# Forty-two products of the identity with zeros per turn, put into TensorE's order in a four-layer transformer kernel

## The chip, the cores and the metric

The kernel runs on one core of one Trainium2 chip. The metric is the device time of one execution in microseconds (us), so less is better. Before the change it is 3342.41 us, the median of three executions (3336.08 to 3346.99). TensorE is called PE here, VectorE DVE and ScalarE ACT. SyncE (SP) issues the DMAs, and GpSimd (POOL) only clears a few tiles at the start.

## The reference, cut to what matters

The input is 16 sequences of 256 tokens with 128 features. Eight stages follow each other, each one a layer norm, the stage and a residual:

```python
x = x + _L0_attn_ref(_layernorm(x, axis=-1), ...)   # causal attention, 16 heads of 8
x = x + _L0_ffn_ref(_layernorm(x, axis=-1), ...)    # 8 experts, top 2, with a capacity
x = x + _L1_attn_ref(_layernorm(x, axis=-1), ...)   # causal attention
x = x + _L1_ffn_ref(_layernorm(x, axis=-1), ...)    # 4-head attention with shared keys, then 8 experts
x = x + _L2_attn_ref(_layernorm(x, axis=-1), ...)   # linear attention
x = x + _L2_ffn_ref(_layernorm(x, axis=-1), ...)    # causal attention, then a gated MLP
x = x + _L3_attn_ref(_layernorm(x, axis=-1), ...)   # attention whose weights come from arccos
x = x + _L3_ffn_ref(_layernorm(x, axis=-1), ...)    # three blocks of quantised linears with low-rank terms
```

## The kernel before, in words

Work is cut into eight passes of two sequences (512 tokens), with the features on the 128 partitions. A pass has a front half (first two layers: `causal0`, `moe0`, `causal1`, `mqa`, `moe1`) and a back half (`linear`, `causal2`, `mlp`, `arccos`, `qlora` and three blocks). There are two regions, `one` and `two`. Each has its own SBUF and four PSUM banks of its own (`one_ps`, `two_ps`). The program has three parts. "fronts" runs the front halves of the first two passes, one in each region. "both" is a loop of six turns; a turn runs the front half of one pass in region `one` beside the back half of an earlier pass in region `two`. "backs" runs the last two back halves.

Every engine's order is written out. Each stage is a generator per engine (`headed_pe`, `mqa_act`, ...) that yields between steps, and `weave` takes steps from the two halves in turn by the numbers of `PE_RUNS`, `ACT_RUNS` and `DVE_RUNS`:

```python
    for i, steps in enumerate(runs):
        for _ in range(steps):
            next(halves[i % 2], None)
```

An engine therefore waits at the head of its own list, and what stands behind the waiting instruction waits too. A step begins with its semaphore waits. All hand-overs between engines go through semaphores that count up.

The places that the change and the prediction touch, by line of the kernel before: L557 and L564 are the two matmuls of a layer norm. L658, L659 and L649 are the projections. L766 and L772 are scores for a softmax's maximum, and DVE's L797 takes the maximum. L837, L843 and L848 are the scores, with ACT's L933 as their exponential, and L862 and L865 multiply by the values. L883 and L910 are linear attention. L1001 and L1008 end an attention stage. L1124, L1132, L1148, L1150 and L1164 are the 4-head attention `mqa`, and L1095 and L1099 are its end. L1257 and L1275 are the arccos attention, whose ACT passes are L1320 and L1322 and whose sums are DVE's L1330. L1595 to L1646 are the experts of `moe0`. L1437 and L1448 spread the routing weights of `moe1`, and L1710, L1717 and L1723 are its experts. L1821 and L1826 are the linears of the blocks. Most of these matmuls take fp32 operands, and each of those stands as two records in the trace: four matmuls of 128 columns are "x8".

`clear_ps` (L894) is a product of the bf16 identity with zeros. It is used four times at the program's start, ahead of everything.

Of the kernel before, what the change touches and what calls it, by code (L numbers as in the profile page):

```python
# [33 lines left out]
P = 128  # L34
# [78 lines left out]
class Signal:  # L113
# [12 lines left out]
    def before(self, turn):  # L126
# [53 lines left out]
    ),  # L180
    "both": (
# [5 lines left out]
    ),  # L187
    "backs": (
# [50 lines left out]
        ("block", "block0"), ("block", "block1"), ("block", "block2")]  # L239

# [239 lines left out]
def build(nc, x_dram, w_dram, qw_dram, out_dram):  # L480
    cols, width = columns()
    with ExitStack() as ctx:
        def sb(name, shape, dt=F32):
            return ctx.enter_context(nc.sbuf_tensor(name, shape, dt))
# [15 lines left out]
        zero_bf, spare = sb("zero_bf", [P, 1], BF16), sb("spare", [P, 1])  # L500
        max_rows = sb("max_rows", [P, GROUPS], F32R)
# [16 lines left out]
        def C(name):  # L518
            return W("const", name)
# [1345 lines left out]
        def run(eng, runs, stage_of, before_back=None):  # L1865


            def half(h, parts, turn):
                return in_turn(parts, turn, {kind: lambda t, s, f=f: f(eng, h, t, s) for kind, f in stage_of.items()})
# [52 lines left out]
        @block.gpsimd  # L1922
        def _(pool):

            for h in (one_front, two_front):
                nc.gpsimd.memset(h.v18[:], 1.0).then_inc(consts_ready, 1)
                nc.gpsimd.memset(h.negm[:], 0.0).then_inc(consts_ready, 1)
                nc.gpsimd.memset(h.v33[:], 1.0).then_inc(consts_ready, 1)
            nc.gpsimd.memset(zero_bf[:], 0.0).then_inc(consts_ready, 1)
            nc.gpsimd.memset(spare[:], 0.0).then_inc(out_stored, 16)  # L1930

        CONSTS = 19
# [11 lines left out]
        def _(pe):  # L1944
            pe.wait_ge(loaded["const"], 16)
            pe.wait_ge(consts_ready, CONSTS)
            for region in (one, two):
                for bank in (2, 3):
# [3 lines left out]
                     "moe1": moe1_pe, "mlp": mlp_pe, "arccos": arccos_pe, "block": block_pe}, lora_pe)  # L1952
# [147 lines left out]
```

## Time and profile before

| | |
|---|---|
| median of three executions | 3342.41 us |
| lowest and highest | 3336.08 and 3346.99 us |
| the profiled execution, span from first to last instruction | 3337.4 us |
| PE busy | 2641.8 us, 79% |
| ACT busy | 1912.7 us, 57% |
| DVE busy | 1763.9 us, 53% |
| mean granted clock of PE | 0.795 of full speed |
| chain that ended last | PE 54%, ACT 19%, DVE 15%, issue 12% |

The profiled execution's own time is its span, 3337.4 us, which is 5.0 us under the median. The row PEclk of the page shows the clock that was granted to PE in each fortieth of the span. It is 1.0 for 2.4 GHz and 0.5 for 1.2 GHz, and figures between are means over both. The chain of work that ended last goes back from the last instruction to what released it, step by step. Busy shares are means over stages with different limits, so a stretch is read by its own row.

### The profile page before, as it was taken

What the parts mean: (1) busy time and instruction counts of PE and PEld (TensorE: products, weight loads), DVE (VectorE), ACT (ScalarE), POOL (GpSimd) and SP (SyncE); (2) the same over time, 40 slices, a digit from 0 to 9 for tenths busy, and PEclk for the clock granted to TensorE, in tenths of its full rate; (3) what the DMA queues carried; (4) which work ended last, traced back from release to release, by engine and by line L of the source; (5) the groups of instructions that cost most, each with busy time, mean ns of one, the idle gap of its engine ahead of it and who ended that gap; (6) DMA issues with size and microseconds to landing.
All of it is one profiled execution on the core that took longest, in us unless ns stands there. A gap on an engine that the chain in (4) does not pass through costs nothing.

```text
span 3337.4 us, 46425 instructions
## 1 busy us (share of the span) xinstructions
PE 2641.8 (79%) x18736; PEld 1529.0 (46%) x18736; DVE 1763.9 (53%) x2698; ACT 1912.7 (57%) x1960; POOL 3.6 (0%) x12
## 2 busy tenths in 40 slices
PE   8999999777997789877898688986889868897215
PEld 4666456343563435534355344553445534453102
DVE  5463574545656355553555545654455544563524
ACT  2433435875358753586445864468534685447994
POOL 0000000000000000000000000000000000000000
PEclk7997989659896588966899668986779867987557
DMA  3000000000000000000000000000000000000000
GB/s 128 2 1 1 20 1 1 1 1 8 1 1 1 1 8 1 1 1 0 8 1 1 1 0 8 2 1 1 0 5 2 1 1 0 4 1 1 0 0 6
DMA packets 4561, 18.68 MB, mean 6 GB/s; under 512 B 608, under 2 KB 864, under 8 KB 3808
## 3 DMA queue, kind: packets, MB, share of 16 engines
q1 hardware_dynamic: 4320, 15.38, 1.2%
q8 instruction: 162, 2.65, 0.3%
q14 instruction: 79, 0.65, 0.1%
HBM read 13.28 MB, written 2.10 MB: 5 GB/s over the span
## 4 chain that ended last, share of the span: by engine, by line
PE 54%; ACT 19%; DVE 15%; issue 12%; DVEq 0%; DMA 0%; ACTq 0%; SPq 0%
ACT back_cosines L1320 6%; PE one_ps L1164 2%; PE two_ps L1275 2%; PE one_ps L862 2%; PE two_ps L910 2%; ACT back_cosines L1322 2%; PE one_ps L1710 2%; DVE back_nsum L1330 2%; PE one_ps L1717 2%; ACT L1320 2%; PE one_ps L766 1%; PE one_ps L1723 1%; DVE back_cosines L1393 1%; ACT L1862 1%; PE two_ps L862 1%
## 5 line engine op out<-in xcount | busy, mean ns | idle before, releaser
L1320 ACT ACTIVATE back_cosines<-back_cosines 128x2048 f32<-128x2048 f32 x256 | 472.2, 1899 | 0.5
L933 ACT ACTIVATE front_scratch<-one_ps 128x1152 f32<-128x1152 f32 x168 | 171.5, 1021 | 225.0 <-PE one_ps L848 224.8
L1322 ACT ACTIVATE back_cosines<-back_cosines,wts 128x2048 f32<-128x2048 f32 x128 | 252.4, 1994 | 41.1 <-DVE back_cosines L1393 40.9
L1330 DVE TENSOR_REDUCE back_nsum<-back_cosines 128x8 f32<-128x2048 f32 x64 | 144.4, 2281 | 234.0 <-ACT back_cosines L1320 234.0
L797 DVE TENSOR_REDUCE front_negm<-one_ps 128x8 f32<-128x1024 f32 (+1 forms) x168 | 204.4, 1220 | 56.6 <-PE one_ps L772 55.5
L837 PE MATMUL one_ps<-ident_bf,mask_q 128*128 128x256 bf16 x480 | 93.3, 302 | 80.5 <-ACT front_scratch L933 69.3
L696 ACT ACTIVATE back_cosines<-two_ps,wts 128x512 fp32r<-128x512 f32 x28 | 19.3, 688 | 224.1 <-PE two_ps L910 224.1
L766 PE MATMUL one_ps<-front_qkr 32*128 32x128 f32 (+1 forms) x896 | 136.5, 414 | 14.1 <-issue 8.9
L1393 DVE TENSOR_SCALAR back_cosines<-two_ps 128x2048 f32<-128x2048 f32 x56 | 128.2, 2290 | 28.5 <-PE two_ps L1257 28.3
L933 ACT ACTIVATE back_cosines<-two_ps 128x1152 f32<-128x1152 f32 (+1 forms) x84 | 86.0, 1024 | 92.0 <-PE two_ps L848 92.0
L766 PEld LDWEIGHTS one_ps<-front_qkr 32*128 32x128 f32 x896 | 96.6, 274 | 88.5 <-DVE front_negm L797 46.3
L1275 PE MATMUL two_ps<-back_cosines,back_vs 128*18 128x256 f32 x896 | 79.5, 505 | 69.0 <-DVE back_vs L1342 69.0
L862 PE MATMUL one_ps<-front_scratch,one_v 128*18 128x256 f32 x896 | 116.7, 424 | 6.1 <-DVE front_split_parts L704 5.7
L772 PE MATMUL one_ps<-mask_q,ident_bf 128*128 128x512 bf16 (+1 forms) x360 | 119.4, 428 | 0.0
L843 PE MATMUL one_ps<-front_qkr 32*128 32x256 f32 (+1 forms) x896 | 105.8, 328 | 0.0
L797 DVE TENSOR_REDUCE back_cosines<-two_ps 128x4 f32<-128x1024 f32 (+1 forms) x84 | 97.9, 1216 | 8.8 <-PE two_ps L772 8.6
L837 PEld LDWEIGHTS one_ps<-ident_bf,mask_q 128*128 128x128 bf16 x480 | 39.2, 103 | 132.7 <-ACT front_scratch L933 92.1
L700 DVE TENSOR_SCALAR front_scratch<-one_ps,wts 128x512 fp32r<-128x512 f32 x77 | 57.4, 746 | 71.6 <-PE one_ps L865 56.0
L910 PE MATMUL two_ps<-back_cosines,two_v 128*18 128x128 f32 x896 | 77.8, 376 | 20.9 <-DVE back_split_parts L704 20.6
L1164 PEld LDWEIGHTS one_ps<-front_v,front_scratch 128*128 128x128 f32 x448 | 85.0, 291 | 13.0 <-issue 13.0
L953 DVE TENSOR_TENSOR back_cosines<-two_ps,wts 128x768 f32<-128x768 f32 (+1 forms) x84 | 72.6, 864 | 34.8 <-PE two_ps L883 34.8
L843 PEld LDWEIGHTS one_ps<-front_qkr 32*128 32x128 f32 x896 | 71.3, 208 | 42.1 <-issue 42.1
(630 smaller groups left out, 5795.1 us busy)
## 6 DMA issues: line engine op xcount, KB each, us to landing
wts<-w_dram SPq DMA_DIRECT2D x1, 4184.0 KB, 15.3
front_xin<-x_dram SPq DMA_DIRECT2D x8, 256.0 KB, 4.2
out_dram<-back_z SPq DMA_DIRECT2D x8, 256.0 KB, 2.1
wts<-w_dram SPq DMA_DIRECT2D x1, 1736.5 KB, 19.1
wts<-w_dram SPq DMA_DIRECT2D x1, 1199.0 KB, 5.3
wts<-w_dram SPq DMA_DIRECT2D x1, 1152.0 KB, 16.5
wts<-w_dram SPq DMA_DIRECT2D x3, 256.0 KB, 5.8
wts<-w_dram SPq DMA_DIRECT2D x1, 516.5 KB, 4.8
```

The costliest lines, as they stand in the source:

```text
L766: nc.tensor.matmul(h.ps[:, j, gi * keys:(gi + 1) * keys], h.q4r[rows(j, QUAD), g0 + gi, b * SEQ + qt * P:b * SEQ + (qt + 1) * P], h.k4r[ro ...
L797: nc.vector.tensor_reduce(into, h.ps[:, js, :].rearrange("p j (g k) -> p j g k", k=keys), AX.X, ALU.max, negate=True).then_inc(h.max_done. ...
L843: nc.tensor.matmul(h.ps[:, k, into], h.k4r[rows(j, QUAD), g, keys], h.q4r[rows(j, QUAD), g, queries], start=False, stop=False, skip_group_ ...
L862: nc.tensor.matmul(h.ps[rows(j, V2), 3, b * SEQ:(b + 1) * SEQ], h.v18[:, 2 * b, GROUPS * j + g, :], h.probs[:, e % 2, k * HEADW:k * HEADW ...
L910: last = nc.tensor.matmul(h.ps[rows(j, V2), 3, b * SEQ + t * P:b * SEQ + (t + 1) * P], h.v18[:, 2 * b + t, GROUPS * j + g, :], h.probs[:, ...
L933: nc.scalar.activation(h.probs[:, e % 2, 0:n * HEADW].rearrange("p (k c) -> p k c", c=HEADW), h.ps[:, 0:n, 0:HEADW], ACT.Exp, scale=float( ...
L1164: last = nc.tensor.matmul(h.ps[:, 3, c:c + MV1], h.probs[:, (e - 1) % 2, w:w + P], h.v33[:, 2 * b + kt, :], start=(kt == 0), stop=(kt == 1 ...
L1275: last = nc.tensor.matmul(h.ps[rows(j, V2), 2 + g2, 0:SEQ], h.vs[:, kt, HPG * g2 + j, :], h.cosines[:, u % 2, w:w + SEQ], start=(kt == 0), ...
L1320: nc.scalar.activation(cosines, cosines, func, scale=scale).then_inc(h.arc_pass.sem, 1)
L1322: nc.scalar.activation(cosines, cosines, func, scale=scale, bias=C(bias)).then_inc(h.arc_pass.sem, 1)
L1330: nc.vector.tensor_reduce(h.nsum[:, kt, :].rearrange("p (g2 j) -> p j g2", g2=2), h.cosines[:, u % 2, kt * 4 * TOK:(kt + 1) * 4 * TOK].rea ...
L1393: nc.vector.tensor_scalar(h.cosines[:, u % 2, kt * 4 * TOK:(kt + 1) * 4 * TOK].rearrange("p (j t) -> p j t", j=HPG), h.ps[:], CLIP, CLIP_L ...
```

## The change

A tile of zeros `zero_f` (fp32) is added, and a table `IDLE_WORK` that says for a step of a half how many products of the fp32 identity with zeros PE issues ahead of it, into which bank and which quarter of it. They always go to bank 3, mostly its last quarter. An entry has two counts: the first are issued before the other half gets its turn, the second after it. Entries of (0, 0) issue nothing and only add a yield. 22 counts are above zero, and they sum to 42 for a front and a back half together: 18 in the front half, 24 in the back half. The numbers of `PE_RUNS` are written anew so that the added yields move nothing. A product has no wait and raises no semaphore.

```diff
 PE_RUNS = {
     "fronts": (
-        1, 1, 1, 1, 1, 1, 1, 1, 1, 1, 2, 2, 2, 1, 2, 2, 5, 1, 5, 2, 1, 1, 2, 1, 2, 1, 2, 1, 2, 1, 2, 1, 2, 2, 2,
+        2, 2, 2, 2, 2, 2, 2, 2, 2, 2, 2, 2, 3, 1, 2, 3, 5, 1, 6, 2, 2, 1, 4, 1, 4, 1, 3, 1, 2, 1, 4, 1, 3, 3, 2,
...
+IDLE_WORK = {
+    "front": {
+        1: (2, 3, (0, 0)), 2: (3, 3, (0, 0)), 3: (3, 3, (0, 0)), 4: (3, 3, (0, 0)), 5: (3, 3, (0, 0)), 9: (3, 3,
+        (0, 0)), 21: (3, 3, (0, 0)), 22: (3, 3, (0, 0)), 23: (3, 3, (0, 4)), 24: (3, 3, (0, 0)), 25: (3, 3, (0,
...
+        3, (0, 0)), 126: (2, 3, (0, 0)), 133: (3, 3, (2, 2)), 134: (3,
+        3, (0, 4)), 135: (3, 3, (0, 0)), 136: (3, 3, (0, 0)), 137: (3, 3, (0, 0)), 138: (3, 3, (0, 0)), 139: (2,
...
+        zero_f = sb("zero_f", [P, 1])
...
+        def with_idle_work(h, steps, work):
+
+            step = 0
+            while True:
+                if step in work:
+                    bank, quarter, times = work[step]
+                    for part, n in enumerate(times):
+                        if part:
+                            yield
+                        for _ in range(n):
+                            nc.tensor.matmul(h.ps[:, bank, quarter * P:(quarter + 1) * P], C("ident"),
+                                             zero_f[:].broadcast_to([P, P]), start=True, stop=True, skip_group_check=True)
+                try:
+                    next(steps)
+                except StopIteration:
+                    return
+                step += 1
+                yield
...
             def half(h, parts, turn):
-                return in_turn(parts, turn, {kind: lambda t, s, f=f: f(eng, h, t, s) for kind, f in stage_of.items()})
+                steps = in_turn(parts, turn, {kind: lambda t, s, f=f: f(eng, h, t, s) for kind, f in stage_of.items()})
+                if idle_work:
+                    return with_idle_work(h, steps, idle_work["front" if parts is FRONT else "back"])
+                return steps
...
+            nc.gpsimd.memset(zero_f[:], 0.0).then_inc(consts_ready, 1)
...
-        CONSTS = 19
+        CONSTS = 20
```

Lines of the kernel from L237 on stand 48 or 49 lines further down in the changed kernel, and from the new helper on 71 or 72 lines further down. The product itself is L1924 there. Three places in PE's order follow. The first is in the loop, early in a turn: `one` takes the maxima of `causal0` while `two` is in its linear attention. PE's order before:

```order
L910 MATMUL two_ps<-back_cosines,two_v 18x128 x6
L876 REGISTER_ALU
L883 MATMUL two_ps<-back_qkr 128x128 x4
L910 MATMUL two_ps<-back_cosines,two_v 18x128 x6
L763 REGISTER_ALU
L766 MATMUL one_ps<-front_qkr 128x128 x8
```

The same place in the changed kernel:

```order
L959 MATMUL two_ps<-back_cosines,two_v 18x128 x6
L1924 MATMUL two_ps<-zero_f,wts 128x128 x2
L925 REGISTER_ALU
L932 MATMUL two_ps<-back_qkr 128x128 x4
L959 MATMUL two_ps<-back_cosines,two_v 18x128 x6
L812 REGISTER_ALU
```

Two products stand between the two linear-attention steps, and all else keeps its place. The second place is in the loop too, a little later, where `two` leaves linear attention (`two_ps` with L1008) and `one` is in its `causal0` scores. PE's order before:

```order
L843 MATMUL one_ps<-front_qkr 128x128 x3
L848 MATMUL one_ps<-front_maxTr,max_rows 128x128 x3
L1008 MATMUL two_ps<-back_xn,wts 128x512
L834 ISA
L837 MATMUL one_ps<-ident_bf,mask_q 128x2x128 x3
```

And in the changed kernel:

```order
L892 MATMUL one_ps<-front_qkr 128x128 x3
L897 MATMUL one_ps<-front_maxTr,max_rows 128x128 x3
L1057 MATMUL two_ps<-back_xn,wts 128x512
L1924 MATMUL one_ps<-zero_f,wts 128x128 x4
L883 ISA
L886 MATMUL one_ps<-ident_bf,mask_q 128x2x128 x3
```

Four products stand ahead of the next score set. The third place is late in a turn, where `one` ends `mqa` (L1164, L1095, L1099) and `two` is in the last value products of arccos (L1275). PE's order before:

```order
L1164 MATMUL one_ps<-front_v_64,front_scratch 128x33 x8
L1275 MATMUL two_ps<-back_cosines,back_vs 18x256 x16
L1156 REGISTER_ALU
L1164 MATMUL one_ps<-front_v_64,front_scratch 128x33 x8
L1095 MATMUL one_ps<-wts,front_scratch 128x128 x4
L1099 MATMUL one_ps<-front_xn,wts 128x512
L1275 MATMUL two_ps<-back_cosines,back_vs 18x256 x16
L564 MATMUL one_ps<-front_sq,wts 128x512
```

And in the changed kernel:

```order
L1213 MATMUL one_ps<-front_v_64,front_scratch 128x33 x8
L1324 MATMUL two_ps<-back_cosines,back_vs 18x256 x16
L1924 MATMUL two_ps<-zero_f,wts 128x128 x4
L1205 REGISTER_ALU
L1213 MATMUL one_ps<-front_v_64,front_scratch 128x33 x8
L1144 MATMUL one_ps<-wts,front_scratch 128x128 x4
L1148 MATMUL one_ps<-front_xn,wts 128x512
L1924 MATMUL one_ps<-zero_f,wts 128x128 x2
L1324 MATMUL two_ps<-back_cosines,back_vs 18x256 x16
L1924 MATMUL one_ps<-zero_f,wts 128x128
L613 MATMUL one_ps<-front_sq,wts 128x512
```

Four, two and one products come in at three points. On ACT, DVE and SP every row stands where it stood, and POOL has one more memset at the start.

## Rows read from the trace of the kernel before

**Rows 1.** The page: its span, PE's clock in forty slices, the chain by engine.
```profile
span 3337.4 us, 46425 instructions
...
PEclk7997989659896588966899668986779867987557
...
PE 54%; ACT 19%; DVE 15%; issue 12%; DVEq 0%; DMA 0%; ACTq 0%; SPq 0%
```

**Rows 2.** Stretches: length; busy PE, PEld, DVE, ACT, POOL; clock; DMA share, GB/s.
```profile
1248.00:1278.70 30.70, 26.98 (x192) 16.02 (x191) 19.71 (x26) 2.47 (x4) 0.00 (x0) 0.50 0.00 1
1278.70:1405.00 126.30, 118.01 (x1085) 76.27 (x1084) 68.59 (x129) 63.73 (x93) 0.00 (x0) 1.00 0.00 1
1405.00:1411.80 6.80, 5.75 (x19) 3.46 (x20) 4.58 (x4) 4.91 (x4) 0.00 (x0) 0.50 0.00 0
1415.20:1469.80 54.60, 38.15 (x243) 19.65 (x243) 28.20 (x29) 52.57 (x33) 0.00 (x0) 0.50 0.00 1
...
1558.60:1565.40 6.80, 4.41 (x22) 1.75 (x26) 5.24 (x9) 1.06 (x2) 0.00 (x0) 0.50 0.00 0
...
1585.90:1592.70 6.80, 5.48 (x8) 2.19 (x8) 4.42 (x6) 5.29 (x6) 0.00 (x0) 0.50 0.00 0
...
309.30:346.80 37.50, 36.48 (x130) 25.96 (x130) 11.56 (x42) 10.60 (x14) 0.00 (x0) 0.50 0.00 0
...
1534.70:1551.80 17.10, 17.10 (x82) 14.87 (x82) 5.86 (x8) 15.31 (x10) 0.00 (x0) 0.50 0.00 1
...
1496.00:1550.00 54.00, 37.54 (x144) 24.21 (x143) 16.35 (x27) 53.55 (x39) 0.00 (x0) 0.53 0.00 0
```

**Rows 3.** Timeline of PE, start and length in us: fp32 matmuls of 128 columns.
```profile
330.85 1.89 PE L1437 MATMUL one_ps<-wts,front_wtok 128*16 128x128 f32 x8
...
1364.96 1.05 PE L1638 MATMUL one_ps<-wts,front_parts 128*128 128x128 f32 x8
1365.85 1.06 PE L1623 MATMUL one_ps<-front_scratch,wts 128*128 128x128 f32 x8
...
1578.04 1.05 PE L1437 MATMUL one_ps<-wts,front_wtok 128*16 128x128 f32 x8 [1.54 <-DVE front_wtok L1570]
```

**Rows 4.** The chain in 1248 to 1279: shares by line, then start, length, what.
```profile
by line: PE two_ps L910 29.1%; PE one_ps L766 14.4%; PE two_ps L883 13.5%; PE one_ps L772 11.4%; PE two_ps L1001 9.7%; DVE back_split_parts L704 9.5%; issue 6.2%; DVE back_cosines L953 3.6%; PE two_ps L920 2.8%; ACT back_cosines L696 2.3%; 
...
1248.93 1.05 PE two_ps L910 x12
1249.98 0.62 PE two_ps L883 x4
```

**Rows 5.** Timeline of PE at full clock; idle before in brackets.
```profile
1282.05 0.50 PE L837 MATMUL one_ps<-ident_bf,mask_q 128*128 128x256 bf16 x3 [0.18 <-ACT front_scratch L933]
...
1361.03 1.05 PE L1623 MATMUL one_ps<-front_scratch,wts 128*128 128x128 f32 x8
...
1367.35 1.06 PE L1406 MATMUL two_ps<-wts,back_xn 128*128 128x8 f32 x8 [0.45 <-DVE back_xn L622]
```

**Rows 6.** Timelines of PE and of ACT at the start of the `mqa` probabilities.
```profile
1529.87 1.23 PE L1148 MATMUL one_ps<-front_qk 32*128 32x256 f32 x4 [1.63 <-DVE front_maxTr L704]
...
1533.40 1.00 ACT L1186 ACTIVATE front_scratch<-one_ps 128x1024 f32<-128x1024 f32 x1
```

**Rows 7.** The chain from 1557 to 1592: start, length, what.
```profile
1557.20 2.28 DVE back_nsum L1330
...
1560.30 1.13 PE one_ps L1095 x4
...
1562.10 2.08 PE one_ps L1099 x2
1564.18 2.52 PE two_ps L1275 x32
...
1587.35 2.07 PE one_ps L1710 x2
```

**Rows 8.** Timeline of PE where five products come in ahead of L557.
```profile
1583.78 1.20 PE L1448 MATMUL one_ps<-front_maxTr,expert_rows 16*128 16x512 f32 x4 [0.91 <-ACT front_qk L1481]
```

More of the change, by code:

```diff
@@ L239 @@
         ("block", "block0"), ("block", "block1"), ("block", "block2")]
+IDLE_WORK = {
+    "front": {
[22 rows of a table added]
+    },
+    "back": {
[18 rows of a table added]
+    },
+}
 def weave(runs, halves):
@@ L1863, in table, with run @@
             in_table[0] = name
-        def run(eng, runs, stage_of, before_back=None):
+        def with_idle_work(h, steps, work):
[15 more added lines that the diff above has]
+                yield
+        def run(eng, runs, stage_of, before_back=None, idle_work=None):
             def half(h, parts, turn):
-                return in_turn(parts, turn, {kind: lambda t, s, f=f: f(eng, h, t, s) for kind, f in stage_of.items()})
+                steps = in_turn(parts, turn, {kind: lambda t, s, f=f: f(eng, h, t, s) for kind, f in stage_of.items()})
+                if idle_work:
+                    return with_idle_work(h, steps, idle_work["front" if parts is FRONT else "back"])
+                return steps
             table(None)
@@ L1951, in _ @@
             run(pe, PE_RUNS, {"norm": norm_pe, "causal": headed_pe, "linear": headed_pe, "mqa": mqa_pe, "moe0": moe0_pe,
-                     "moe1": moe1_pe, "mlp": mlp_pe, "arccos": arccos_pe, "block": block_pe}, lora_pe)
+                     "moe1": moe1_pe, "mlp": mlp_pe, "arccos": arccos_pe, "block": block_pe}, lora_pe, IDLE_WORK)
         @block.scalar
```

67 rows, old and new, of tables (IDLE_WORK, PE_RUNS) are left out of this document.

## The prediction

> **What bounds the kernel now.** I read the page first, its row of PE's clock and its chain [rows 1]. PE is 54% of the chain over a span of 3337.4 us, and the clock wanders between 5 and 9 tenths with the same pattern in every turn of the loop. So the question is where PE is both on the chain and at the low level. I took the turn from 1213.8 to 1623.4 as the sample, cut it where the granted clock changes, and asked for busy times by stretch [rows 2]. The reader is to see three kinds. From 1278.7 to 1405.0 the clock is 1.00 (2.4 GHz) and PE is busy 118.01 of 126.30 us: nothing can be won there, and PE is the bound. In 1415.2 to 1469.8 and in 1496.0 to 1550.0 the clock is at or near 0.50 (1.2 GHz), but ACT is busy 52.57 of 54.60 and 53.55 of 54.00: a faster PE would wait for ACT. Only the third kind pays: 1248.0 to 1278.7, 1405.0 to 1411.8, 1558.6 to 1565.4 and 1585.9 to 1592.7 all have 0.50, PE busy four fifths of the time or little less, and ACT and DVE with room. Then I looked up each insertion in the changed order, found the instructions around it in the trace, and read the idle time in front of the one behind it.
>
> **What a product costs.** The trace has no fp32 product of 128x128 with 128 columns of zeros, but real ones of that shape. Four of them are "x8". L1638 starts at 1364.96 and L1623 behind it at 1365.85: 0.89 us for four, 0.22 us each at 2.4 GHz [rows 3]. L1437, of the same columns, takes 1.89 us at 0.50 and 1.05 at 1.00 for four, 0.84 us more, so 0.43 us each at 1.2 GHz. A product behind which PE waits anyway costs nothing; behind which it doesn't, its full price. It has no wait and signals nobody, so nothing else queues. 42 per turn are 9.2 us at full clock and 18.1 us at the low level. Zero operands could only make this cheaper in power, not in time: I use the price of the real ones.
>
> **Part by part, one turn.** What comes back is half of PE's time in a stretch that turns from 1.2 to 2.4 GHz, as far as PE is on the chain. Which stretches turn can't be read from the trace of before; I bound each.
>
> A, 1248.0 to 1278.7: two products behind L910 with nothing idle there, since L883 starts at 1249.98 where L910 ends [rows 4]. They cost 2 x 0.43 = 0.86 us for certain. PE's lines make 81% of the chain (29.1, 14.4, 13.5, 11.4, 9.7 and 2.8%), 24.8 of 30.7 us. At full clock throughout that would be 12.4 less, but DVE has 19.71 us of work, so at most 11.0 come back. At the low end nothing does. Work of the same kind let the clock fall at 1248.0, so I expect a short lift: a fifth of the 11.0, 2.2, less 0.86, and I take +1.5. This is the least sure term, from -0.9 to +10.1.
>
> B, 1405.0 to 1411.8: one product shortly before (0.22). PE is busy 5.75 us there; full clock returns at most 2.9. I take +0.8.
>
> C, the single product at 1461 (low, 0.43): ACT hides its cost and most of its gain. +0.5, from 0 to 2.
>
> D, eight products ahead of L1148 at 1529.87, where PE is idle 1.63 us for DVE [rows 6]. At 1.2 GHz they take 3.4 us, so L1148 starts 1.8 us later. ACT's exponential behind it starts at 1533.40, with ACT full before it; the score set is two groups of some 1.2 us, so it ends near 1532.3 before and near 1534.1 after; 0.7 us would show if the clock stays low, and none if it rises. The gain is bounded by ACT, which stays full until 1550.0 [rows 2]. I take 0, from -0.7 to +3 (only if PE were still fast for the last L1164 and L1275 behind ACT's end).
>
> E, 1558.6 to 1565.4: four products at 1555.7, in front of L1164, whose result DVE wants only after its 2.28 us sum (L1330) [rows 7], so their 0.88 us are hidden. If they hold the clock up, L1095 (1.13), L1099 (2.08) and the first half of L1275 run at full clock: 4.4 us busy become 2.2. Two more products ahead of L1275 cost 0.44. +1.6, from -1.1 to +1.8.
>
> F, 1585.9 to 1592.7: L1710, L1717 and L1710 of `moe1` stand on the chain at 1.2 GHz, the first with 2.07 us [rows 7]; PE is busy 5.48 us [rows 2], and at full clock half of it, 2.7, comes back. The five products at 1581.8 fill 1.1 us against 0.91 us idle [rows 8]: 0.2 lost. +2.2 before that, from -0.2 to +2.7 with it.
>
> G, the products in the long stretch at full clock: four with 0.18 us idle to fill, 0.88 - 0.18 = 0.70; two ahead of L837 in the `causal2` scores and two ahead of L1623 with none idle, 0.44 each; single ones ahead of L1406, where 0.45 us are idle [rows 5], and ahead of L1222, alike, hidden. PE is the bound there: -1.6, almost certain.
>
> The rest of the turn's products (1566 to 1578) stand where PE is idle longer than they take, as the 1.54 us ahead of L1437 [rows 3]: 0. What is late next where a low stretch goes is DVE in A, and nothing new in E and F, whose chain is PE, ACT and DVE by turns.
>
> Sum of a turn: 1.5 + 0.8 + 0.5 + 0 + 1.6 + 2.2 - 0.2 - 1.6 = 4.8 us. Six turns: 29 us. In "fronts", eight products stand ahead of the `mqa` of `two`, whose low stretch 309.3 to 346.8 is PE alone (36.48 of 37.50 us) with no ACT to wait for [rows 2]; at most 18 us come back there, and the other products cost some 3. I take +5 net. In "backs" most of the low time is ACT's, so 0. In all 34 us: 3337.4 - 34 = 3303.4 for the profiled execution, and since the median of before stands 5.0 us above it, 3308 us.
>
> **Two rules of the Trainium skill.** From 1534.7 to 1551.8 PE is busy 17.10 of 17.10 us, and the clock is 0.50 all the while [rows 2]. The Trainium skill, page "TensorE: Matmul & The Clock Gate", section "Why this matters for your kernels", says that PE kept busy continuously gets to full clock. The trace differs: by that rule this stretch would have been fast already; by the row a PE that never idles can stay at the low level, so filling idle time is no promise of a faster clock. The same page, section "PE-mode transpose", says that transposes, products with an identity, don't count as busy for the clock in the same way. No run shows whether a plain matmul on the identity falls under it; by that rule the case of the slower rival below would hold.
>
> **The rivals.**
> Slower: the products don't raise the clock, or raise it where ACT holds the chain. Then only prices are left. Per turn: A 0.86, B 0.22, E 0.44 and one more of 0.22, F 0.2, G 1.6, a last 0.4 for C and D, together 4.0 us, six turns 24 us; "fronts" and "backs" have 84 products, at the same 0.095 us a product 8 us. 3342.4 + 32 = 3374 us. It decides as soon as a turn gets back less than 4.0 us from the clock. For it: in 1534.7 to 1551.8 a full PE is not enough, and A starts with a sure loss. Against it: E and F lie right behind a stretch at 1.00 and need it held only a little longer.
> Much faster: A stays at 2.4 GHz to its end and so does the `mqa` in "fronts". That is 8.6 us more a turn, 52 us, and up to 13 more in "fronts": 3308 - 65 = 3243 us. For it: PE is 81% of the chain there. Against it: the same work let the clock fall.
> No change: E and F give 3.8 us a turn, A and G take 2.5 of it back, the rest moves into waits: 1.3 x 6 = 8 us, 3334 us. The edit does move PE's order as it says, so that it does nothing is no case of its own.
>
> **How the numbers follow.** A measurement of this kernel tells a change from none beyond about 0.3%, that is outside 3332 to 3352 us. I give the forecast 0.53, the much faster case 0.14, no change 0.14, slower 0.19. Faster is 0.53 + 0.14 = 0.67. The forecast's own range is 3285 to 3330 us: A alone moves a turn by -2.4 to +8.6, the others by about 2 either way, and they don't all fall out alike in six turns. The range for 8 in 10 goes on to 3262 below, half way into the much faster case, and to 3360 above, half way into the slower one.
>
> **What the profile after would show.** The products, L1924, with 672 records in all, mean spacing 0.11 us a record at full clock. If I am right: in a turn the granted clock is 1.00 where F stands (the first L1710 takes about 1.1 us, not 2.07), and where E stands (L1099 about 1.1 us). The stretch of A is shorter by 1 to 4 us, with DVE waited for more often. ACT's full stretches are as long as before, whatever the clock does in them. The long full-clock stretch is longer by 1 to 2 us. The mean granted clock is above 0.82. I am wrong to the slow side if the clock is low in E and F as before, and to the fast side if A is at 1.00 throughout.

## The result, and the profile after

The changed kernel takes 3356.78 us, the median of seven executions (3353.01 to 3364.34), against 3342.41 us of before on the same chip (seven, 3334.25 to 3347.15). The ratio is 1.0041 with a 95% interval from 1.0026 to 1.0056. It is slower by 14 us, and the forecast was 3308.

The page of the changed kernel answers to [rows 1]: its span, PE's busy time, the clock in forty slices, and the chain by engine.

```profile
span 3358.6 us, 47776 instructions
...
PE 2709.0 (81%) x19408; PEld 1621.0 (48%) x19408; DVE 1765.0 (53%) x2698; ACT 1913.1 (57%) x1960; POOL 3.6 (0%) x13
...
PEclk7998879769896688966889668996789867988558
...
PE 57%; ACT 18%; DVE 14%; issue 11%; DVEq 0%; DMA 0%; ACTq 0%; SPq 0%
```

PE is busy 67 us longer, and its share of the chain went up from 54% to 57%. The mean granted clock is 0.810 against 0.795 (the forecast asked for more than 0.82), so the products did raise the clock, and the kernel is slower all the same. The question is therefore where the clock rose and where it fell.

I cut the changed kernel where its clock changes, as in [rows 2] (columns: stretch, length, busy PE, PEld, DVE, ACT and POOL, granted clock, DMA share, GB/s). The copy of `handed` into `back_x` (L638 before, L687 now) is a good mark for the start of a turn. Two turns start at 816.8 and 1225.3.

```profile
816.80:845.30 28.50, 23.66 (x174) 13.11 (x174) 19.12 (x25) 14.19 (x19) 0.00 (x0) 0.92 0.03 10
845.30:872.60 27.30, 24.31 (x187) 13.70 (x185) 17.85 (x23) 1.41 (x3) 0.00 (x0) 0.50 0.00 1
1225.30:1244.70 19.40, 15.81 (x76) 8.00 (x77) 10.06 (x14) 13.50 (x18) 0.00 (x0) 0.85 0.05 15
1244.70:1292.50 47.80, 43.91 (x299) 26.14 (x298) 29.49 (x37) 4.07 (x6) 0.00 (x0) 0.50 0.00 1
1292.50:1422.20 129.70, 121.01 (x1115) 79.27 (x1114) 71.08 (x131) 64.28 (x92) 0.00 (x0) 1.00 0.01 1
...
1548.50:1569.00 20.50, 20.50 (x115) 16.05 (x111) 5.87 (x8) 14.97 (x10) 0.00 (x0) 0.50 0.00 1
1569.00:1575.80 6.80, 4.29 (x30) 3.59 (x31) 6.60 (x8) 0.60 (x1) 0.00 (x0) 1.00 0.00 0
1592.90:1606.60 13.70, 11.58 (x36) 5.22 (x35) 7.11 (x9) 8.52 (x10) 0.00 (x0) 1.00 0.00 0
```

The last row is F (the letters A to G are the stretches of the forecast), and the one ahead of it is the first half of E. F is at 1.00 now, as the forecast wanted. In E the low stretch has moved and is not gone. Here it is just behind the row, and L1148 (L1099 of [rows 7], 2.07 us there) takes 1.30 us in this turn and 1.97 in the second one (a stretch, then PE's timeline):

```profile
1575.80:1579.20 3.40, 3.40 (x29) 1.67 (x31) 1.37 (x4) 0.63 (x1) 0.00 (x0) 0.50 0.00 0
...
1159.21 1.97 PE L1148 MATMUL one_ps<-front_xn,wts 128*128 128x512 f32 x2 [0.69 <-ACT front_xn L1153]
...
1574.96 1.30 PE L1148 MATMUL one_ps<-front_xn,wts 128*128 128x512 f32 x2 [0.69 <-ACT front_xn L1153]
```

Over the six turns L1148 takes 1.30 to 2.07 us, where the forecast wanted 1.1. F's first product takes 1.12 or 1.13 us in all six, but in two of them the clock falls again for 3.4 us soon behind it.

The first four rows above are A in two turns. In the first of them PE's clock holds for 28.5 us and A's low stretch is 27.3 us. In the second it falls after 19.4 us, and the low stretch is 47.8 us. The trace of before has the same two patterns, the long one in its last turn only (2445.6):

```profile
1219.20:1248.00 28.80, 24.07 (x176) 13.18 (x176) 19.43 (x25) 14.20 (x19) 0.00 (x0) 0.91 0.03 11
...
2445.60:2466.50 20.90, 17.39 (x86) 8.64 (x86) 10.85 (x15) 13.52 (x18) 0.00 (x0) 0.83 0.01 2
2466.50:2510.90 44.40, 40.50 (x287) 23.44 (x285) 28.68 (x36) 3.44 (x5) 0.00 (x0) 0.50 0.00 1
```

I call this an early fall. From the mark to A's first L1001 (L1050 now), the six turns take, in us:

| | turn 1 | 2 | 3 | 4 | 5 | 6 |
|---|---|---|---|---|---|---|
| before | 55.9 | 56.1 | 56.1 | 56.1 | 56.1 | **61.6** |
| changed kernel | **64.3** | 57.3 | **62.7** | **62.2** | **62.1** | 57.3 |

Bold turns fell early. So A costs 1.2 us in an undisturbed turn, and an early fall 5 us more. The changed kernel has four of them in its profile where before has one.

The account of the two profiled executions, taken between the same DVE instructions, closes: A has +23.9 us over the six turns (7 of price, about 17 of early falls by the table), G has +8.0 (1.7 in an undisturbed turn), all the rest of the loop has -18.1, fronts +1.9, backs +5.5. The sum is +21.2 us, the difference of the spans.

Two products in A and what follows them (columns: start, length, engine, line, operation, tiles, idle time before):

```profile
1260.47 1.05 PE L959 MATMUL two_ps<-back_cosines,two_v 128*18 128x128 f32 x12 [0.74 <-DVE back_split_parts L753]
1261.45 1.22 PE L1924 MATMUL two_ps<-zero_f,wts 128*128 128x128 f32 x4
1262.61 0.69 PE L932 MATMUL two_ps<-back_qkr 32*128 32x128 f32 x4
```

From the first product to L932 (L883 of [rows 4]) it is 1.16 us, so 0.58 us each at 1.2 GHz, not the 0.43 taken from [rows 3]. The chain through E and F has them too (start, length, what):

```profile
1574.96 1.30 PE one_ps L1148 x2
1576.26 0.85 PE one_ps L1924 x4
...
1595.17 1.31 PE two_ps L1924 x10
...
1603.41 0.86 PE one_ps L1759 x2
```

The first L1759 (L1710 of [rows 7], 2.07 us there) takes 0.86 us, so F did get its clock. But about 3.3 us of products (10.2% of the chain from 1575 to 1608) stand on the path in this stretch, where the forecast put 0.6. Standing on the path is not the same as costing time, though: from the start of L613 (L564 before) at 1580.4 to that of the first L1759 it is 20.6 us in all six turns, against 20.8 in four turns of before and 21.7 in the other two.

### The profile page after: what moved, and what is told of

Same layout as the page of the kernel before. It is cut to its first block, busy times and chain, and to the rows that moved or that the text cites. A ratio compares the mean times of both kernels' runs of the same rounds, so it can differ in the third digit from the quotient of the medians.

```text
span 3358.6 us, 47776 instructions
## 1 busy us (share of the span) xinstructions
PE 2709.0 (81%) x19408; PEld 1621.0 (48%) x19408; DVE 1765.0 (53%) x2698; ACT 1913.1 (57%) x1960; POOL 3.6 (0%) x13
## 4 chain that ended last, share of the span: by engine, by line
PE 57%; ACT 18%; DVE 14%; issue 11%; DVEq 0%; DMA 0%; ACTq 0%; SPq 0%
ACT back_cosines L1369 6%; ACT back_cosines L1371 2%; PE one_ps L1213 2%; PE two_ps L959 2%; PE one_ps L911 2%; PE two_ps L1324 2%; PE one_ps L815 2%; DVE back_nsum L1379 2%; PE one_ps L1766 2%; ACT L1369 2%; PE one_ps L821 2%; PE one_ps L1759 2%; PE one_ps L1772 2%; PE two_ps L606 1%; ACT L1911 1%
## 5 line engine op out<-in xcount | busy, mean ns | idle before, releaser
L745 ACT ACTIVATE back_cosines<-two_ps,wts 128x512 fp32r<-128x512 f32 x28 | 19.3, 688 | 245.0 <-PE two_ps L959 245.0
L815 PE MATMUL one_ps<-front_qkr 32*128 32x128 f32 (+1 forms) x896 | 144.1, 432 | 11.6 <-issue 8.9
L749 DVE TENSOR_SCALAR front_scratch<-one_ps,wts 128x512 fp32r<-128x512 f32 x77 | 57.5, 747 | 75.8 <-PE one_ps L914 60.3
L621 ACT ACTIVATE back_sq<-two_ps 128x512 f32<-128x512 f32 x49 | 29.3, 597 | 103.6 <-PE two_ps L606 102.8
```

The lines of the kernel that those rows point to most:

```text
L815: nc.tensor.matmul(h.ps[:, j, gi * keys:(gi + 1) * keys], h.q4r[rows(j, QUAD), g0 + gi, b * SEQ + qt * P:b * SEQ + (qt + 1) * P], h.k4r[ro ...
```

## The experiments

Each kernel was timed in five rounds beside the kernel before on the same chip. The ratio is to that. "Count" means the entries of `IDLE_WORK`. The order of all other instructions is that of the changed kernel, except where a diff adds some. Line numbers of these kernels lie one to nine above those of the changed kernel. Two theories are weighed. By the price theory a product costs its time or wins clock where it stands, and nothing else moves. By the timing theory how long A stays fast also depends on when a turn arrives, so what is won or lost anywhere moves the early falls.

### One group of products at a time

`only_g`, `only_ef`, `ef_loop`, `bcd_loop`, `a_only`, `behind_l910` and `turn_start` keep one group and set the other counts to zero; `a_filled` has thirty products of its own in A and ahead of it. All but `only_g` and `only_ef` also keep fronts and backs free of products (cut to what matters):

```diff
-                        for _ in range(n):
+                        for _ in range(n if on else 0):
...
-                    return with_idle_work(h, steps, idle_work["front" if parts is FRONT else "back"])
+                    return with_idle_work(h, steps, idle_work["front" if parts is FRONT else "back"], turn.register is not None)
```

**G alone.** 

> Of the products only the ten of a turn in the long stretch at full clock (G). They can bring nothing where they stand. Price theory: plus 1.7 us a turn and 3 us outside the loop, 3342 + 13 = 3355 us, with A as before. Timing theory: 3355 us plus about 6 us for each turn in which A's clock falls early, up to 3391 us.

Measured: 3340.29 us, ratio 1.0003 (0.9987 to 1.0018). Its rows of the long stretch at full clock and of a whole turn:

```profile
1278.70:1408.50 129.80, 120.90 (x1112) 78.92 (x1111) 71.48 (x131) 64.93 (x93) 0.00 (x0) 1.00 0.01 1
...
1219.80:1629.20 409.40, 332.85 (x2360) 193.67 (x2360) 219.44 (x336) 240.14 (x246) 0.00 (x0) 0.80 0.01 2
```

PE is the bound there as in [rows 2], and between the same DVE instructions G takes 1.7 us longer, as forecast. Yet its first five turns take 409.0 to 410.1 us against 409.2 in the usual turn of before (the last turn of each kernel is some 2.6 us shorter behind F). The 1.7 us are given back behind G in most turns: from 196 to 251 us behind the mark it takes 53.5 us in four of the six, where before takes 55.0 to 56.6. Both theories fail here. The price is real and the kernel doesn't pay it.

**B, C and D alone.** 

> Only the ten products of B, C and D, in the loop; eight of them stand ahead of L1148 (D). The prediction gave B +0.8, C +0.5, D 0: 8 us less, ratio 0.998. If ACT holds that part of the turn whatever PE's clock is: 1.000.

Measured: 3332.41 us, ratio 0.9977 (0.9957 to 0.9996). This is the size of the forecast's B, C and D, and the lowest ratio of all that ran. Its turns don't bear out the terms, though. Two take 406.6 us, but `start_and_fronts` (below), whose loop has none of these ten products, has a turn of 406.5 us too, and the fifth turn of before takes 407.1:

```profile
1224.40:1630.90 406.50, 330.32 (x2344) 191.35 (x2344) 219.51 (x335) 240.33 (x246) 0.00 (x0) 0.81 0.01 2
```

Three more turns take 409.1 to 409.6 us, as the usual turn of before. What its profile has less than that of before lies mostly in the last turn, which doesn't fall early (406.8 against 413.4 us).

**E and F alone, with fronts and backs, and in the loop only.** 

> Of the products only those of E and F and the few between them (1555 to 1582 in a turn of the kernel before). Price theory: E and F give 2.0 to 2.5 us a turn and nothing else moves, 3342 - 14 = 3328 us. Timing theory: the same gain of about 14 us, plus about 6 us for every turn in which A's clock falls early; with none 3328, with all six 3364 us. If E and F give nothing by themselves: 3342 us.

> The products of E and F and between them, in the loop only. Where they also stood in fronts and backs, a turn took 406.5 us against 409.2 in the usual turn of before, yet backs took 491 us against 478. If the products in backs are the cost: 6 x 2.7 = 16 us less than before, ratio 0.995, less 5 us of that for each turn whose A falls early beyond the one of before. If backs is longer for another reason: ratio about 1.001, as with the products everywhere.

Measured: 3342.04 us, ratio 1.0025 (1.001 to 1.004), and 3345.67 us, ratio 1.0009 (0.9987 to 1.0031). Here are three turns of the second in a row, and below them the two parts of A in the second and the third turn:

```profile
403.50:810.50 407.00, 334.10 (x2376) 195.14 (x2376) 219.18 (x336) 240.38 (x246) 0.00 (x0) 0.81 0.02 6
810.50:1225.60 415.10, 343.70 (x2376) 201.33 (x2376) 219.91 (x336) 240.47 (x246) 0.00 (x0) 0.78 0.01 2
1225.60:1632.10 406.50, 332.03 (x2376) 195.00 (x2376) 219.49 (x336) 240.35 (x246) 0.00 (x0) 0.81 0.01 2
...
810.50:830.80 20.30, 17.15 (x86) 8.81 (x86) 10.92 (x15) 13.51 (x18) 0.00 (x0) 0.83 0.04 14
830.80:875.20 44.40, 40.51 (x285) 23.54 (x284) 28.64 (x36) 3.57 (x6) 0.00 (x0) 0.50 0.00 1
1225.60:1254.10 28.50, 23.72 (x174) 13.10 (x174) 19.16 (x25) 14.19 (x19) 0.00 (x0) 0.92 0.03 11
1254.10:1281.50 27.40, 23.96 (x186) 13.27 (x182) 18.43 (x24) 2.06 (x3) 0.00 (x0) 0.50 0.00 1
```

This is the clearest picture of the case. The turns take 407.0, 415.1 and 406.5 us, though they have the same instructions; the second falls early. In the profile this repeats every three turns, and the mean over the six is 409.1 us, against 409.7 in before: the gain is nearly gone. What differs at the start of the early turn is when the clock rose: 6.7 us behind the mark at 810.5, 4.6 us behind the one at 1225.6. Where the clock changes doesn't move along with the turn, so a turn that arrives earlier has its high time at other instructions.

How much of a short turn is E and F is read between the same DVE instructions. E's stretch (336 to 346 us behind the mark) takes 9.6 us in all six turns, and 9.4 to 10.3 in before: no gain that can be told from its spread. F's (360 to 381 us) takes 19.3 us in two turns and 20.8 in four, and 21.0 to 21.2 in before. So F gives 1.8 us where the clock stays up for all of it, and 0.2 elsewhere. The turn of 406.5 us is one of the four. Of its 2.7 us under the usual 409.2, 1.5 lie from 193 to 336 us, ahead of the first product of E, and `start_and_fronts` reaches 406.5 with no product of E and F in its loop.

**The two pairs of A.** 

> Only the two products at a turn's start and the two in A behind L910, in the loop. The prediction took A for +1.5 us a turn (a gain). By the profiles so far A is 1.2 us longer with them at either clock: 3342 + 7 = 3349 us, ratio 1.002, and no lift of the clock in A's low stretch. If they do lift it: ratio 0.997 or less. If they also make A fall early: 1.005 and more.

> Only the two products in A behind L910, in the loop. If this pair is the cause: about 20 us slower than before, ratio 1.006, with A 58 us or more from the turn's marker (the copy of handed to back_x) to the first L1001 in most turns, against 56.1. If the other pair is: price alone, 6 x 1.2 = 7 us, ratio 1.002.

> Only the two products at a turn's start, in the loop, ahead of the first L557, where PE is idle 4.55 us. Their price is hidden: if nothing else follows, ratio 1.000. If they are the cause of the 0.76%, because the clock then rises later behind them: ratio 1.004 to 1.006, and the clock at 1.00 from 7 to 8 us behind the marker on, against 4.1 to 4.8 in the usual turn of before.

Measured: both pairs 3363.41 us, ratio 1.0076 (1.005 to 1.0102). Behind L910 alone 3336.32 us, ratio 0.9994 (0.9973 to 1.0015), with A at 57.1 to 57.5 us in every turn: the price of 1.2 us and no lift. At the turn's start alone 3355.31 us, ratio 1.0058 (1.0033 to 1.0083). I had not expected two products in 4.55 us of idle time to cost this. PE's timeline at the seam, of before and of `turn_start`:

```profile
1213.44 1.72 PE L1826 MATMUL two_ps<-back_sq,weff 128*128 128x512 f32 x2
...
1219.71 2.07 PE L557 MATMUL two_ps<-back_x,wts 128*128 128x512 f32 x2 [4.55 <-DVE back_x L638]
```

```profile
1217.75 1.12 PE L1876 MATMUL two_ps<-back_sq,weff 128*128 128x512 f32 x2
1223.61 0.76 PE L1925 MATMUL two_ps<-zero_f,wts 128*128 128x128 f32 x2 [4.73 <-issue]
1226.69 0.80 PE L1925 MATMUL two_ps<-zero_f,wts 128*128 128x128 f32 x2 [2.32 <-issue]
1227.27 1.91 PE L607 MATMUL two_ps<-back_x,wts 128*128 128x512 f32 x2
```

Between the two products PE waits 2.32 us for nothing that the profile shows ("issue"). From the end of the last L1876 to the first L607 it is 6.6 us or more (8.4 here) in all five seams of `turn_start`, and 4.5 to 5.1 us in before. The clock comes up later with it, 7.1 to 7.7 us behind the mark in the five turns that follow, against 4.1 to 4.8 in the first five of before. But the changed kernel has both pairs and no such stall: its seams are 4.6 to 4.8 us. So I ran the pair again behind fronts with their 36 products.

> The two products at a turn's start in the loop, and the 36 products of fronts ahead of it, which only lie before the loop in time and in the code. If the stall between the two products hangs on where the loop's code lies: it is gone, the first L607 starts 4.7 us behind the turn's last L1876 product as in the changed kernel, and the time is 1.000 to 1.002 of before. If it comes of the products themselves: 6.6 us as in turn_start, and 1.006 again.

Measured: 3344.28 us, ratio 1.0012 (0.9997 to 1.0027). Its seam:

```profile
1218.51 1.73 PE L1876 MATMUL two_ps<-back_sq,weff 128*128 128x512 f32 x2
1222.62 1.20 PE L1925 MATMUL two_ps<-zero_f,wts 128*128 128x128 f32 x4 [2.37 <-issue]
1224.93 2.08 PE L607 MATMUL two_ps<-back_x,wts 128*128 128x512 f32 x2 [1.12 <-DVE back_x L688]
```

The stall is gone in all five seams (4.6 to 4.9 us), though the loop's instructions are the same. What changed is only what stands before the loop. The three kernels with this pair and no product in fronts (`turn_start`, `a_only` and `after_loop`, the last two at 6.5 to 6.8 us) stall in every seam, and the four with both (the changed kernel, `no_g`, `after_hold` and this one) in none. That speaks for where the loop's first instructions lie, though no run changed that alone, and why the issue stops is not shown. The difference of 0.46% between the two kernels, whose intervals don't overlap, goes with the stall, and a part of the loss of `a_only` and `after_loop` can be that.

**A filled.** 

> Products only in A and ahead of it, thirty per turn of the loop: 4 ahead of L658 of linear, 2 ahead of the front's q, 1 and 1 after, then 2 at each of eleven places between the groups of L883 and L910. Much-faster rival of the prediction: A stays at 2.4 GHz, up to 11 us a turn back, less some 5 us of price: a turn 6 us shorter, 3342 - 36 = 3306 us. If they can't hold the clock: 22 x 0.43 = 9.5 us a turn of price less the idle time they fill (about 3 us in A): 3342 + 40 = 3382 us, with A's low stretch 27 us or more in every turn.

Measured: 3403.48 us, ratio 1.0178 (1.0164 to 1.0192). A stretch of A, and two places in it:

```profile
1275.70:1305.20 29.50, 26.95 (x178) 17.64 (x172) 15.20 (x16) 1.38 (x2) 0.00 (x0) 0.50 0.00 1
```

```profile
1277.79 1.22 PE L1925 MATMUL two_ps<-zero_f,wts 128*128 128x128 f32 x4
1278.94 1.05 PE L960 MATMUL two_ps<-back_cosines,two_v 128*18 128x128 f32 x12
...
1281.79 1.06 PE L1925 MATMUL two_ps<-zero_f,wts 128*128 128x128 f32 x4
1282.78 0.69 PE L933 MATMUL two_ps<-back_qkr 32*128 32x128 f32 x6
```

PE is busy 26.95 of 29.50 us with products among the work, and the clock is 0.50. So the much faster rival fails even with A filled: A is 11 us longer a turn. The loss is above my 40 us because a product costs 0.50 to 0.58 us at this level, not 0.43.

### The changed kernel with a group taken out

**Without G.** 

> The changed kernel without the ten products of a turn that stand in the long stretch at full clock (the term G). Price theory (only prices and clock gains, each where its products stand): minus 1.7 us a turn and some 3 us outside the loop, 3357 - 13 = 3344 us, and the low stretch inside A stays 41.0 us or more in four of six turns. Timing theory (how long A stays fast depends on when a turn arrives, and G's 1.7 us help to decide that): the low stretch in A is back at 27.3 to 30.7 us in most turns, 3357 - 13 - 24 = 3320 us.

Measured: 3346.18 us, ratio 1.0027 (1.0007 to 1.0048), from 3332.91 to 3370.01. Without G the ratio is 0.14% lower than with it, where the price theory asked for 0.4% and the timing theory for 1.1%, and the intervals overlap. In its profile one turn of six falls early, but twelve executions spread over 37 us, and all of its interval is above 1. So G alone is not what makes the changed kernel slower, and this run shows no more.

**Without both pairs of A.** 

> The changed kernel without the two products in A behind L910 and without the two at a turn's start. Theory that these products themselves make the clock of A fall early: the low stretch in A is 27.3 to 30.7 us in all turns, 3357 - 6 (their price) - 24 = 3327 us. Price theory: 3357 - 6 = 3351 us with four long stretches. Timing theory: between the two; the long stretches come in other turns than in the changed kernel, not in none.

**Without the pair at the start.** 

> The changed kernel without the two products at a turn's start, the pair behind L910 kept. Without both pairs the ratio was 0.9999, with both 1.0041. If the pair behind L910 makes that difference (1.2 us a turn of price and the early falls): 1.003 to 1.004. If the pair at the start does: 1.000 to 1.002.

Measured: without both 3338.89 us, ratio 0.9999 (0.9986 to 1.0012), without the start pair 3354.01 us, ratio 1.0035 (1.0016 to 1.0055). So the pair behind L910 makes most of the loss of the changed kernel, though alone it made none. Both profiles have two early falls, so these don't explain the difference by themselves.

**Products in the loop only.** 

> The changed kernel with its products in the six turns of the loop only; fronts and backs are as before. The profile of the changed kernel has fronts 1.9 us and backs 5.5 us longer than before. Theory that those are prices of the products there: 7 us less than the changed kernel, 3350 us against before at 3342 (ratio 1.002). Theory that fronts and backs vary by as much without any product: no difference from the changed kernel, ratio 1.004.

Measured: 3355.14 us, ratio 1.0046 (1.0033 to 1.0059). This run doesn't decide, as its five seams have the stall, 10 us in all. Backs took 478.4 or 478.5 us in eight kernels without products there, before among them, but 486.1 to 489.7 in four others without. It took 483.9 to 491.4 in the seven with the change's products in backs, and 477.2 in `bf_hold_all` (below), which has only the hold's there. Whether the 5.5 us of the changed kernel are price or another early fall stays open.

### Holding the clock through A

Two products ahead of each group of row-picking products, behind its waits, just ahead of where A falls early:

```diff
+            hold(h, turn, s)
             spread_pe(h, 0, ("q_of_high", "q_of_low"), h.q_ps)
...
+            hold(h, turn, s)
             spread_pe(h, 2, ("k_of_high", "k_of_low"), h.k_ps)
+
+        def hold(h, turn, s):
+            if turn.register is not None and s in ("linear", "causal0"):
+                for _ in range(2):
+                    nc.tensor.matmul(h.ps[:, 3, 0:P], C("ident"), zero_f[:].broadcast_to([P, P]),
+                                     start=True, stop=True, skip_group_check=True)
```

> The changed kernel with two more products ahead of each of the four row-picking products' groups of linear and causal0 (L734 and L735, offsets 14 to 18 us in a turn, just ahead of where A falls early), each behind its wait, eight per turn in the loop. Timing theory (A falls early where what PE does at these offsets lets the clock go): the low stretch in A is 27 to 31 us in all turns, 4 x 5 = 20 us back, less the products' price of at most 8 x 0.22 x 6 = 11 us: 3357 - 9 to 3357 - 20 us. Price theory: 11 us slower than the changed kernel, 3368 us, and low stretches of 41 us and more remain.

> Only the eight products ahead of the row-picking groups, in the loop. They cost up to 8 x 0.22 x 6 = 11 us. Timing theory: the early falls of A that before has in some turns are gone, which gives 5 us back where there was one: ratio 0.999 to 1.002, every turn 409 to 411 us. Price theory: ratio 1.003.

> The products of E and F and between them in the loop, and two more ahead of each of the four groups of row-picking products of linear and causal0. Timing theory: E and F gain 2.7 us a turn and no A falls early, so the gain is kept: 6 x (2.7 - 0.6) = 13 us less than before, ratio 0.996, and a narrower spread than the 3329 to 3365 us of E and F alone. Rival (a turn's mean stays near 409 us whatever is won, because what is won at one place is lost at another): ratio 1.000 or above, with another stretch longer.

> All products of B to F in the loop, and the eight that hold A; none at a turn's start, in A and in G. Timing theory: as with E, F and the hold, or 1 us a turn better if B, C and D give what the prediction took: ratio 0.994 to 0.997. If they only cost: 0.997 to 1.000.

> All products of B to F in the loop, and the two ahead of each row-picking group in linear and causal0 everywhere, in fronts and backs too. It ran at ratio 0.9987 with the hold in the loop alone; backs took 486 us there and 478.5 where the clock held at its start. If the hold works in backs as in A: 5 to 8 us less in most executions, ratio 0.996 to 0.998, the first below 1 beyond doubt. If backs loses time elsewhere: 0.999 to 1.000.

The changed kernel with the hold: 3350.33 us, ratio 1.0011 (0.9994 to 1.0028). Its turn whose clock rose late, which would fall early without the hold:

```profile
1634.60:1665.10 30.50, 27.60 (x192) 15.55 (x192) 20.26 (x26) 14.50 (x19) 0.00 (x0) 0.89 0.03 10
1665.10:1692.40 27.30, 24.41 (x184) 14.07 (x184) 17.17 (x23) 2.06 (x3) 0.00 (x0) 0.50 0.00 1
```

In `ef_loop` the turn at 810.5, with the same 6.6 to 6.7 us from the mark to the rise, had 20.3 us ahead of the fall and 44.4 us behind it. Here the clock holds for 30.5 us. No turn of the five kernels with the hold fell early in its profile. Eight more products a turn made the changed kernel faster, from a ratio of 1.0041 to one of 1.0011, though their intervals overlap by a little. That is what the timing theory says, and the price theory has it the other way.

But the rival in `ef_hold`'s expectation holds too. Alone, the hold gives 3338.40 us, ratio 1.0001 (0.9983 to 1.0019). With E and F 3349.01 us, ratio 1.0013 (0.9998 to 1.0028), although no A falls early. Every other turn takes 411.3 or 411.7 instead of 407.6 us, with A's low stretch ending 61 us behind the mark instead of 56, and 1.8 us lost right behind A. With B to F it gives 3339.21 us, ratio 0.9987 (0.9965 to 1.0009), and held everywhere 3331.21 us, ratio 0.9992 (0.9967 to 1.0016), from 3325.74 to 3357.21. The last has the lowest median of all, but its interval holds 1.

## Why the prediction was wrong

- **The price of a product.** Right at 2.4 GHz: G costs 1.7 us a turn against 1.6. At 1.2 GHz among products of other shapes it is 0.58 us, not 0.43. The rest of the turn's products, taken at 0, did cost nothing: they are on the chain now, and L613 to the first L1759 takes 20.6 us where it took 20.8. The forecast's list leaves out the two products at a turn's start; in the changed kernel they cost nothing that shows (1.0035 without them, 1.0041 with them, and the intervals overlap).
- **A, +1.5.** This is the term that failed most. "So I expect a short lift: a fifth of the 11.0" has no support in any run. The pair behind L910 lifts nothing and costs 1.2 us, and with 22 products there the clock falls only 3 us later than in before and then stays at 0.50 for 34.1 us in five turns of six. Even an undisturbed turn lies below the lower bound of -0.9, and over the profile A costs 4 us a turn, with early falls.
- **B, C, D, +1.3.** The size came out, perhaps by luck: `bcd_loop` gains 0.23%, 7.7 us, where the terms gave 8, with an interval that reaches to 0.04%. Its turns of 406.6 and 409.1 to 409.6 us are lengths that turns without these products have too. In most turns of before, B's low stretch is 3.4 us long, as it still is in `bcd_loop`; the sample turn had 6.8. The eight products of D took 3.6 us in the changed kernel and cost nothing that shows, as forecast.
- **E and F, +1.6 and +2.0.** F was right in its mechanism and too large: between the same DVE instructions its stretch takes 19.3 us in four turns of the changed kernel and 20.8 in two, against 21.0 to 21.2, so 1.3 us a turn on average. E failed. Its step "L1095 (1.13), L1099 (2.08) and the first half of L1275 run at full clock" held for L1095 alone (0.66 us in five turns of six): L1099 took 1.30 to 2.07 us, a low stretch of 3.4 us or more stayed in every turn, and E's stretch takes 9.6 us in five turns against 9.4 to 10.3 before. All of the loop behind G gives 3.0 us a turn in the changed kernel, where the terms had 4.9.
- **"Sum of a turn ... Six turns: 29 us."** This is the step that broke. It takes the six turns as alike and the terms as independent. What a turn wins or loses shifts what follows against the moments at which the clock changes. In `ef_loop` every third turn takes 415 us, 6 above the usual one, G's 1.7 us are given back in most turns before they end, and a kernel with B to F and the hold loses 4 to 5 us in two turns of six, from the end of A on. The trace of before showed it: its last turn takes 413.4 us, with A at 61.6, and its fifth 407.1. The prediction says that the clock has "the same pattern in every turn of the loop", takes one turn as the sample and doesn't compare it with the others.
- **"I take +5 net" in fronts.** No run bears it out. Fronts took 402.7 us in the changed kernel and 400.8 in before, though the low stretch of 37.5 us became one of 30.7. Without any product there it took 394.9 to 407.8 us in the profiles of eleven kernels, so two microseconds say little.
- **The slower rival** said that only prices would be left, 3374 us. The prices are there, but the clock did rise. The result lies between it and no change, and the early falls are a mechanism that none of the rivals named.

The Trainium skill, page "TensorE: Matmul & The Clock Gate", section "Part 1: The HAM clock gate", warns that the number of slow matmuls of one and the same kernel changes from run to run with the phase of the gate at its start. The runs fit it: 35 executions of before in one study go from 3323.4 to 3356.4 us, and the twelve of `ef_loop` from 3328.8 us at a mean clock of 0.807 to 3364.7 us at 0.793. It puts the effect of the first ramp under 1% of a kernel. The whole range of before is 1% too, but here it isn't the first ramp alone: turns of one execution differ by up to 8.6 us.

What stays open: why the pair behind L910 costs nothing alone and some 0.35% among the others; why the issue of PE stops between two products at the start of a loop in some layouts; and what share of the loss is in backs. Open too is why E's low stretch moved and didn't go. My account of A by early falls rests on profiles of one execution each, and the medians over twelve confirm only its direction (`after_hold`).

## What to carry to other kernels

Before adding up what an edit gives per turn, compare all turns of a trace: if turns with the same instructions have different lengths and their clock falls at different places, gains of 1 to 3 us per turn don't add, and the sum needs a term for what a shift does to the next turn. Compare a stretch before and after between the same instructions of another engine, and only in turns whose clock changes at the same places: the length of a whole turn here says little of what was changed in it. Look whether a low stretch is gone or has only moved. Don't expect a few products between dependent small ones at the low level to lift the clock (A here), and take the price from a place with the same neighbours. Time a variant in ten executions or more, since one profile shows only one way in which the clock's changes met the turns.

## What was unexpected of the hardware

- Two products, 1.1 us of work, in 4.55 us of idle time made the loop's first matmul 2 us late in `turn_start` and not in `start_and_fronts`, which differs only ahead of the loop, with PE idle on "issue" for 2.32 us between them.
- Plain products of the fp32 identity with zeros can raise the granted clock: with five of them ahead, F's first product (L1759) took 1.12 us instead of 2.07 in all six turns. But PE busy 20.50 of 20.50 us (1548.5 to 1569.0) and 26.95 of 29.50 us (`a_filled`) stayed at 0.50.
- The mean granted clock rose from 0.795 to 0.810 and the time rose with it; within one kernel it is the other way round, a lower clock goes with a longer time.
